# An LSTM step with the forget and output gates computed by stationary weight tiles instead of through a transpose

## The reference

```python
xW = jnp.einsum('ntd,dg->ntg', x, Wx) + b        # Wx, Wh: (256, 1024), gates i, f, o, g
def step(carry, xw_t):
    prev_h, prev_c = carry
    a = xw_t + prev_h @ Wh
    i = sigmoid(a[:, :H]);      f = sigmoid(a[:, H:2*H])
    o = sigmoid(a[:, 2*H:3*H]); g = tanh(a[:, 3*H:])
    next_c = f * prev_c + i * g
    next_h = o * tanh(next_c)
x = x + lstm(x, h0=cond, Wx, Wh, b)
x = x + ((x * ys) @ weight) * d                  # ys = cond / 16, d = rsqrt((ys*ys) @ (weight*weight) + 1e-8)
```

## Time and profile before

| | |
|---|---|
| median of three runs | 2174.21 us |
| the profiled execution | 2174.8 us, its span 2172.7 us |
| first `rec` matmul | at 26.62 us |
| last product of the loop | at 2153.76 us |
| one step in the middle | 2.07 us |
| TensorE, VectorE, ScalarE, GpSimd busy | 75%, 58%, 36%, 10% of the span |

### The profile page before, as it was taken

The page is one execution under the profiler, slowest core; times in us unless marked ns, Lnnn a source line. Parts: engine busy times, 40 slices in busy tenths (PEclk is TensorE's granted clock), DMA queues, the critical chain, the costliest instruction groups (busy, mean ns, idle before and its releaser), DMA issues.

```text
span 2172.7 us, 201141 instructions
## 1 busy us (share of the span) xinstructions
PE 1619.4 (75%) x88232; PEld 1333.5 (61%) x88232; DVE 1269.2 (58%) x12316; ACT 784.8 (36%) x4100; POOL 215.3 (10%) x1289
## 2 busy tenths in 40 slices
PE   5777777777777777777777777777777777777777
PEld 4666666666666666666666666666666666666665
DVE  3555555555555555555555555555555555555554
ACT  2333333333333333333333333333333333333332
POOL 0110101010101101010101011010101010101100
PEclk9999999999999999999999999999999999999999
DMA  2000000000000000000000000000000000000001
GB/s 84 0 0 0 0 0 0 0 0 0 0 0 0 0 0 0 0 0 0 0 0 0 0 0 0 0 0 0 0 0 0 0 0 0 0 0 0 0 0 39
DMA packets 4427, 6.67 MB, mean 3 GB/s; under 512 B 1090, under 2 KB 2882, under 8 KB 4420
## 3 DMA queue, kind: packets, MB, share of 16 engines
q1 hardware_dynamic: 3872, 5.51, 0.7%
q10 hardware_dynamic: 548, 1.05, 0.1%
HBM read 4.46 MB, written 2.10 MB: 3 GB/s over the span
## 4 chain that ended last, share of the span: by engine, by line
PE 54%; DVE 30%; ACT 9%; issue 5%; DMA 0%; SPq 0%; POOLq 0%; POOL 0%
PE pA L193 53%; DVE pT L295 13%; DVE junk L299 11%; ACT gates L158 9%; DVE hst L307 5%; DVE gates L299 1%; PE pO L247 1%; DMA w_sb<-in_w_dram 0%; PE pO L168 0%; SPq L102 0%; PE pA L182 0%; PE pO L200 0%; DVE ores L315 0%; DVE wsq L275 0%; PE pA L175 0%
## 5 line engine op out<-in xcount | busy, mean ns | idle before, releaser
L193 PE MATMUL pA<-wh_sb,hst 128*2 128x64 f32 (+1 forms) x65536 | 1106.3, 219 | 529.9 <-DVE hst L307 529.0
L193 PEld LDWEIGHTS pA<-wh_sb,hst 128*2 128x2 f32 (+1 forms) x65536 | 922.3, 90 | 806.5 <-DVE hst L307 803.1
L295 DVE STREAM_TRANSPOSE pT<-pA 128x64 f32<-128x64 f32 x2048 | 543.2, 265 | 629.1 <-PE pA L193 557.8
L158 ACT ACTIVATE gates<-pT 128x8 f32<-128x8 f32 x2048 | 375.7, 183 | 1220.3 <-DVE pT L295 1182.0
L299 DVE CUSTOM_DVE_ANT_0 junk<-gates 128x4 f32<-128x4 f32 x4096 | 508.9, 161 | 77.5
L163 ACT ACTIVATE tanhc<-gates 128x2 f32<-128x2 f32 x2048 | 418.8, 204 | 131.9
L307 DVE TENSOR_TENSOR hst<-tanhc,gates 128x4 f32<-128x4 f32 x2048 | 338.4, 165 | 169.5 <-ACT tanhc L163 153.2
L182 PE MATMUL pA<-wx_sb,xr 128*8 128x64 f32 (+1 forms) x16448 | 419.3, 220 | 1.9 <-issue 1.9
L168 PE MATMUL pO<-wh_sb,picks 128*32 128x128 f32 x2096 | 398.1, 274 | 0.0
L299 DVE DVE_READ_ACCUMULATOR2_ANT gates<- 128x1 f32 x4096 | 336.5, 82 | 0.0
L182 PEld LDWEIGHTS pA<-wx_sb,xr 128*8 128x8 f32 (+1 forms) x16448 | 293.9, 94 | 2.2 <-issue 2.2
(11 more groups left out here) (26 smaller groups left out, 9.0 us busy)
## 6 DMA issues: line engine op xcount, KB each, us to landing
outT_dram<-ores SPq DMA_DIRECT2D x8, 256.0 KB, 2.5
xh<-in_xT_dram SPq DMA_DIRECT2D x6, 320.0 KB, 7.7
wx_sb<-in_Wx_dram SPq DMA_DIRECT2D x1, 1024.0 KB, 5.4
wh_sb<-in_Wh_dram ACTq DMA_DIRECT2D x1, 1024.0 KB, 7.8
w_sb<-in_w_dram SPq DMA_DIRECT2D x1, 256.0 KB, 8.1
xh<-in_xT_dram SPq DMA_DIRECT2D x2, 64.0 KB, 7.7
bias_sb<-in_bT_dram ACTq DMA_DIRECT2D x2, 2.0 KB
condT<-in_condT_dram ACTq DMA_DIRECT2D x1, 2.0 KB, 5.6
```

The lines of the kernel that those rows point to most:

```text
L158: act.activation(gates[:, j, :, 0:3 * G].rearrange("p b (a q c) -> p a q b c", a=PAIR, q=PAIR)[:, :, :, :, 0], pT[j][:, 0:PAIR * Q].rearra ...
L193: last = pe.matmul(into(st, j, c, M), hst[:, st, k, lo:lo + M], chunk(wh_sb[:, k, :], c, j, pair), start=False, stop=True, skip_group_chec ...
L295: dve.transpose(pT[j][:, 0:PAIR * Q], pA[st][j][:, 0:PAIR * Q]).then_inc(turned_ready[j], 1)
```

## The change

Gates f and o no longer go through the transpose. For them the operands change places: a tile of 32 weight columns is stationary, and the two columns of h of this step stream past it (`still`), so that the sum comes out with units on partitions, in a new buffer `pS` of four banks (f and o, halves 0 and 1). Gates i and g keep the old way (`turned`), with one pair instead of two. A step has 4 `turned` and 8 `still` calls of four matmuls each, 96 instructions instead of 64. ScalarE has one activation for f, one for i and g together, and one for o, for each half. The x part of f and o is summed for four steps at a time into `pX` (`sum_x`, in a free part of the bank of `pT[0]`), and VectorE carries it with the bias into `pS` once in four steps (`carry_x`), between the two products. The x part of i and g is filled as before, but all of it behind the last step of a block, as there is one set now. The loop's body is 4 steps, 256 bodies. The fillers are gone. GpSimd adds h to x after every step. h is written once, not twice.

```diff
+    TURNED = (I_, G_)
+    STILL = (F_, O_)
     T = 4
-    BODY = SETS * T
-    NBODY = SEQ // BODY
+    NBODY = SEQ // T
...
+        pS = ctx.enter_context(nc.psum_tensor("pS", [P, PAIR * K, 512], F32))
+        pD, pX, pO = pA[0], pT[0][:, AT_X:AT_X + PAIR * K * ROWS], pA
...
         @block.gpsimd
...
+            with pool.Fori(0, NBODY) as it:
+                pool.wait_ge(filled, it + 1)
+                spread(bass.ds(it * T + T, T))
+                for s in range(T):
+                    for j in range(K):
+                        pool.wait_ge(h_ready[j], it * T + (s + 2))
+                    at = h_slot((s + 1) % T)
+                    now = xh[:, :, :, bass.ds(it * T + s, 1)]
+                    pool.tensor_tensor(now, now, hst[:, :, at:at + B].unsqueeze(3), ALU.add).then_inc(xh_ready, 1)
         @block.scalar
...
+            act.dma_start(bias_col[:, :], bC[:, F_ * K:(O_ + 1) * K]).then_inc(bias_loaded, 16)
...
+                for t in range(T):
+                    cols = slice(B * t, B * (t + 1))
+                    for j in range(K):
+                        act.wait_ge(fsum_ready[j], it * T + (t + 1))
+                        act.activation(gates[:, j, :, AT_F], pS[:, j, cols], ACT.Sigmoid)
+                        act.wait_ge(turned_ready[j], it * T + (t + 1))
+                        act.activation(gates[:, j, :, 0:AT_G + 1:AT_G].rearrange("p b q -> p q b"),
+                                       pT[j][:, 0:PAIR * Q].rearrange("p (q r) -> p q r", q=PAIR)[:, :, cols],
                                        ACT.Sigmoid).then_inc(gates_ready[j], 1)
                     for j in range(K):
-                        act.wait_ge(cell_ready[j], it * BODY + (s + 1))
+                        act.wait_ge(osum_ready[j], it * T + (t + 1))
+                        gate = act.activation(gates[:, j, :, AT_O], pS[:, K + j, cols], ACT.Sigmoid)
+                        if t == T - 1 and j == K - 1:
+                            gate.then_inc(o_ready, 1)
+                        act.wait_ge(cell_ready[j], it * T + (t + 1))
                         act.activation(tanhc[:, j, :], gates[:, j, :, AT_C], ACT.Tanh, scale=2.0).then_inc(tanh_ready[j], 1)
         @block.tensor
...
+            def sum_x(n, k):
+                for c in range(G):
+                    last = pe.matmul(pX[c * Q:(c + 1) * Q, n * ROWS:(n + 1) * ROWS], tile(wx_sb[:, k, :], c, n % K, STILL[n // K]),
+                                     xp[:, k, :], start=(k == 0), stop=(k == K - 1), skip_group_check=True)
+                return last
+            XSUMS = [(n, k) for n in range(PAIR * K) for k in range(K)]
+            XSHARE = [XSUMS[0:3], XSUMS[3:6], XSUMS[6:8]]
+            def turned(t, j, k):
+                lo, M = ROWS * t, B * (t + 1)
+                for c in range(G):
+                    last = pe.matmul(pA[j][c * Q:c * Q + M, 0:PAIR * Q].rearrange("p (g u) -> p g u", u=Q), hst[:, k, lo:lo + M],
+                                     two(wh_sb[:, k, :], c, j, G_), start=False, stop=True, skip_group_check=True)
+                return last
+            def still(t, g, j, k, cs=range(G)):
+                n = STILL.index(g) * K + j
+                for c in cs:
+                    last = pe.matmul(pS[c * Q:(c + 1) * Q, n, B * t:B * (t + 1)], tile(wh_sb[:, k, :], c, j, g),
+                                     hst[:, k, h_slot(t):h_slot(t) + B], start=False, stop=True, skip_group_check=True)
                 return last
...
             with pe.Fori(0, NBODY) as it:
...
+                for t in range(T):
+                    pe.wait_ge(h_ready[0], it * T + (t + 1))
+                    turned(t, 0, 0)
+                    turned(t, 1, 0)
                     if t == 0:
+                        pe.wait_ge(x_carried, it + 1)
+                    still(t, F_, 0, 0, range(0, G // 2))
+                    pe.wait_ge(h_ready[1], it * T + (t + 1))
+                    turned(t, 0, 1).then_inc(sums_ready[0], 1)
+                    still(t, F_, 0, 0, range(G // 2, G))
+                    still(t, F_, 0, 1).then_inc(fsum_ready[0], 1)
+                    turned(t, 1, 1).then_inc(sums_ready[1], 1)
+                    still(t, F_, 1, 0)
+                    still(t, F_, 1, 1).then_inc(fsum_ready[1], 1)
+                    for j in range(K):
+                        still(t, O_, j, 0)
+                        still(t, O_, j, 1).then_inc(osum_ready[j], 1)
+                    if t < T - 1:
+                        if t == 0:
+                            pe.wait_ge(xp_ready, it + 2)
+                        pe.wait_ge(gates_ready[0], it * T + (t + 1))
+                        for n, k in XSHARE[t]:
+                            last = sum_x(n, k)
+                        if t == T - 2:
+                            last.then_inc(x_summed, 1)
+                    else:
+                        pe.wait_ge(turned_ready[1], it * T + T)
                         for j in range(K):
+                            fill_bias(j)
+                        for j in range(K):
+                            for k in range(K):
+                                last = fill_x(j, k)
                         last.then_inc(filled, 1)
-                    filler()
...
         @block.vector
...
+            def carry_x():
+                dve.tensor_tensor(pS[:, :, 0:ROWS], pX.rearrange("p (n r) -> p n r", r=ROWS),
+                                  bias_col[:, :].unsqueeze(2).broadcast_to([P, PAIR * K, ROWS]), ALU.add).then_inc(x_carried, 1)
...
+                for t in range(T):
+                    if t == 0:
+                        dve.wait_ge(xh_ready, it * T + (T - 1))
                     if t == T - 1:
+                        dve.wait_ge(xh_ready, it * T + T)
...
+                    at = h_slot((t + 1) % T)
+                    for j in range(K):
+                        dve.wait_ge(tanh_ready[j], it * T + (t + 1))
+                        dve.tensor_tensor(hst[:, j, at:at + B], tanhc[:, j, :], gates[:, j, :, AT_O], ALU.mult).then_inc(h_ready[j], 1)
+                        if t == T - 1 and j == 0:
+                            dve.wait_ge(x_summed, it + 2)
+                            dve.wait_ge(o_ready, it + 1)
+                            carry_x()
```

168 lines of the change are left out of this document (59 added, 109 removed).

## The result

The kernel after takes **2091.46 us** (median of four runs, 2087.31 to 2107.85), the kernel before 2175.03 us in the same session (2173.67 to 2176.11). The ratio is 0.963 with a 95% interval of 0.958 to 0.968: 84 us less, where 177 had been forecast. The profiled execution took 2090.74 us, its span is 2088.9 us. Ratios, here and in the table of the experiments, leave disturbed runs out and medians do not, which matters for two kernels there, the split fill (one run of 2086.06 us) and the moved wait (one of 5912.42 us).

The account below looks back on a forecast made before the run. Bound: one closed ring of 1024 steps through the engines, no engine full. 2174.8 less 1024 x 0.173 = 177, plus 4.5 for body ends, less 5 at the start, gives 1997; predicted 1998 us, range 1945 to 2260.

Parts of the forecast that it names:

- The ring: Closed chain through TensorE, VectorE and ScalarE in every step: forecast 1.90 us a step against 2.071, 173 ns less.
- The j=0 ring: The chain through half j=0 of h: forecast to bound the 1.90 us step, with half j=1 having 57 ns to spare.
- F0: ScalarE's forget-gate activation for half 0: forecast to start 432 ns after TensorE starts on half j=1 of h.
- that a two-column matmul has 53 ns less latency than a 64-column one: TensorE to ScalarE: 235 ns from the start of a two-column matmul, where a 64-column one has 285.
- The first rival (55 ns a pass): TensorE: a `still` pass costs a full 55 ns; 100 ns a step less than before, 2072 us; chance 12%.
- the second (no overlap on ScalarE): ScalarE's eight activations of a step start 0.168 us apart; step 74 ns longer than before, 2250 us; chance 10%.
- TensorE's loop end and the reads of the next body lie behind it too; I leave up to 100 ns a body, 26 us, in the range and nothing in the sum.: TensorE, behind the fourth step's x fill: up to 100 ns a body, 26 us, allowed in the range, nothing in the sum.
- the cover thin, 76 ns: Fourth step: the x fill ends 76 ns before TensorE starts on the new h; gone at 55 ns a pass (2 us).
- The two more waits of VectorE fall in its gap ahead of transpose 0: VectorE, steps 0 and 3: the added waits fall in idle time ahead of the first transpose, with no cost in the sum.
- a body's end: Loss per body kept from the old kernel's GpSimd copy beside cell 0: 128 more bodies x 35 ns, 4.5 us.
- The clock: Rival: TensorE falls to the lower clock level, 2565 us if for the whole run, deciding from 31% of steps; chance 18%.
- The carry: VectorE's `carry_x` between the products, once in four steps: 0.12 us, hidden; upper bound 88 ns a body, 22 us.

Follow-up runs that it names:

- the split fill: Kernel after, with the fill of each half in the fourth step waiting only for its own transpose: 2049.32 us, ratio 0.941.
- the moved wait: Kernel after, with VectorE's wait for GpSimd in the fourth step moved from ahead of transpose 0 to ahead of cell 1: 2110.28 us, ratio 0.964.
- the new order: Kernel after with filler, split fill and absorbed wait, plus both `turned` calls of half 1 ahead of the forget gate: 1989.36 us; with TensorE's loop turned too, 1986.51 us.
- both experiments on it: Kernel after, VectorE's fourth-step wait for GpSimd either moved ahead of cell 1 (2110.28 us) or taken by a memset behind transpose 1 (2106.83 us).
- the run with filler, split and absorbed wait: Kernel after with a filler in steps 0 to 2, each half's fill behind its own transpose, and a memset taking VectorE's wait: 2011.59 us, ratio 0.925.

## Why the prediction was wrong in size, and what in it was right

**The ring was right, step by step.** Median times of an ordinary step, forecast and measured, in ns: last matmul of sum 0 behind the first load 356 and 347; to transpose 0 287 and 297; to cell 0 517 and 508; to tanh0 285 and 288; to product 0 237 and 237; to the first load 217 and 215. Sum 1.899 and 1.892. Also the late ones: O1 111 behind tanh0 (forecast 111), tanh1 107 behind O1 (107). The j=0 ring binds, as put. F0 starts 61 ns later than forecast, which cost nothing here and cost 35 ns in the new order. Its last matmul is early (448 ns behind the first load, forecast 475), but the activation comes 322 ns behind it and not 235: that a two-column matmul has 53 ns less latency than a 64-column one is not what the runs show.

**The first rival (55 ns a pass) and the second (no overlap on ScalarE) are wrong.** A `still` pass adds 26 ns beside `turned` ones and takes 30 to 42 in a row, so 27 was too little for most of them, but the output gate does not wait for its sum. Activations start down to 70 ns apart, in the new order to 56, less than I took. The Trainium skill, "ScalarE: Activation LUTs", What ACT_TABLE_LOAD costs, has back-to-back activations overlap by about 93 ns; the trace agrees. The overlap, duration of the first less the distance of the starts, is 204 - 111 = 93 ns for O1 behind tanh0 and 177 - 70 = 107 for O0 behind IG1, and in the new order 155 - 56 = 99 for tanh1 behind O1. The Trainium skill, "Advanced Engine Details and Errata", The Read-Write Bubble, has the access latency exposed between instructions of ScalarE; that small ones do not overlap, as the prediction took from it, is contradicted by all three.

**The step that failed first: "TensorE's loop end and the reads of the next body lie behind it too; I leave up to 100 ns a body, 26 us, in the range and nothing in the sum."** It costs 144 ns a body as long as it stands behind the fill. I had called the cover thin, 76 ns, and then not gone on. The fill itself was no later than forecast: its last matmul starts 94 ns behind product 0, 121 ahead of the 215 at which T0 is due. But 266 ns pass from that matmul to the next load, and 94 + 266 = 360. The sentence should have been a term.

**"The two more waits of VectorE fall in its gap ahead of transpose 0" failed too.** The gap is there, and in step 0 the second wait costs nothing. In the fourth step the wait that ends the gap has an instruction of its own, and the transpose is 72 ns later. In the kernel after this is hidden by the fill in the end (both experiments on it left the body unchanged), so body for body the whole excess of 7.792 - 4 x 1.892 = 0.224 us belongs to the ring from transpose 1 through the fill and the loop end. Forecast for a body's end: 35 ns more than before for 128 bodies.

**The clock was mis-sized, and in kind.** I priced the low level as a rival for the whole run (2565 us, "decides from 31% of the steps"), and as nothing in the forecast. It came in short stretches, in 47 of 253 bodies, at 1.03 us each. The prediction also miscounts here: `rec` has 8 calls a step and not 16 (its 16 passes are right), and of the 24 new passes 16 stream two columns, two thirds and not half. No term of the sum used this.

**The ledger.** From 1997.3 (the forecast for the profiled execution: 2174.8 - 177 + 4.5 - 5) to 2090.7: clock 48.3; body ends 256 x 0.224 - 4.5 = 52.8; ordinary step 1.892 instead of 1.902, the mean of before (16.60 / 8) less 0.173: -10.2; start and tail 2.6, since the first product comes 5.7 us earlier and the tail is 0.5 shorter, but the first body loses 5.9 us to the low clock and to reading instructions where before lost 2.0, so that 2.4 are won instead of 5. Sum 93.5, and the difference is 93.4.

**The carry** was hidden, as forecast, but by the loop end beside it, not by its own slack: it makes product 1 some 75 ns late, where 57 were to spare. With the loop end moved away the step at its place is 25 ns too long, in the new order 57.

## What to carry to other kernels

When a ring gets shorter, recount what stands once a body beside it: an engine's loop end was some 240 to 270 ns here in which it issued nothing, and belongs where that engine idles (turning one engine's loop by a step moves it without touching the others). Undo hidden costs in pairs before calling one harmless: here the fill, the loop end, the double wait and the carry each covered another, and single edits moved time from one step to the next. If the new work of TensorE is of another kind than the old, price the low clock level as a share of the bodies and look for it in windows; one cheap unused matmul in its idle gaps was worth 49 us.

## What the runs showed of the hardware

- A loop body of 992 matmuls and 992 loads on TensorE is read from memory in each round (18.87 MB on the instruction queue, 41% "issue" in the chain); 689 and 689 are not (0.10 MB). The run took twice the time, with the granted clock at 0.520. Where between the two it changes was not tried.
- Four steps unrolled around TensorE's loop came with 2.9 us more at the start, 1.4 in the last step and 2.3 behind it, much of it at the lower clock level. How much is the reading of instructions is open.
- Loop ends: 266 ns from TensorE's last fill matmul to the next load in the kernel after, 236 in the run with filler, split and absorbed wait; on VectorE 273 from the branch to the next register instruction.
- A pass of two streamed columns and 32-column weights over the four column tiles adds 26 ns beside 64-column passes, and takes 30 ns at the start of a row of such passes (new order) and 42 over a row of 12 (10 ns an instruction). Its result is taken up 298 to 322 ns behind its start, that of a 64-column matmul 286 to 298.
- Two waits ahead of one VectorE instruction cost 72 ns where the wait that ends last is the one with an instruction of its own, and nothing where that one is the long fulfilled (step 0).
- The kernel before keeps the upper clock level without its fillers, at 65% TensorE busy; the kernel after does not at 86%. What decides is open, and so is why the count of slow bodies differs between kernels (23 to 78 without a filler) and between executions of one.
